# Another order and another cut of the sort in a graph-attention kernel: six groups, border steps moved, square roots issued earlier

## The chip, the cores and the metric

The kernel runs on one core of a Trainium2 chip. The metric is the device time of one execution in microseconds (us). The engines' names in the profile: PE is TensorE (PEld its weight loads), DVE is VectorE, ACT is ScalarE, POOL is GpSimd, SP is SyncE, which only issues DMAs here.

## What is computed

A graph with 6250 nodes of 96 values and 106,250 edges (both directions of 50,000, and a loop at each node), sorted by dst. For every edge the softmax-like weight of its four heads is computed and the weighted values are summed at the node `src`; then a layer norm.

```
q = (x[src] @ qW).reshape(e, 4, 24)
k = (x[dst] @ kW).reshape(e, 4, 24)
v = (x[dst] @ vW).reshape(e, 4, 24)
w = exp(clip(einsum('ehd,ehd->eh', q, k), -10, 10))
norms = segment_sum(w, src)[src]
res = segment_sum((w / (norms + 1e-8))[:, :, None] * v, src)
out = layernorm(x + (x + res))
```

## The kernel before

**Tiles.** Edges are wanted in order of src, cut into 49 blocks of 128 nodes. An edge tile is 128 edges of one block; `U` = 5 tiles make an iteration, and there are 176 iterations. In iteration m (function `tiles` of each engine, one after the other by hand) POOL has gathered the edges' k and v rows from the table `kv_table` in DRAM, one indirect DMA per tile (L475, five per iteration); PE turns a one-hot matrix (`ps_t`, L635), multiplies it with the block's q (`ps_q`, L609) and later the transposed one with the weighted values (`ps_r`, L623); DVE multiplies q by k (L1059), reduces (L1078), clips (L1086), weighs (L1068), builds the one-hot matrix (L1049) and adds to the block's sums (L1041); ACT takes the exponential (L720) and copies the one-hot matrices (L727, L733). The engines run one to two iterations apart. POOL may be ahead by `R` = 8 buffers and by `Y` = 6 results: before gather n it waits for `s_wv` at n - 7 and `s_res` at n - 5.

**The sort.** The gathers need the addresses `dst_s` of their edges, in the order of src. The 850 columns of 125 edges are sorted in groups of `GC` columns. Group g is sorted while the tile iterations of group g - 1 run. One group needs, in this order:
- ranking, mostly on DVE, in named pieces: `mark0` to `mark3` (49 comparisons, L800), `tally` (PE counts the marks, ACT copies), `pay` (L810 to L818), `pair0` to `pair2` (L824 to L830), `count` (waits for the tally's copies and for PE), `base`, `bounds`, `sel0` to `sel6` (L942, L946), `table`, `tree`, `own`, `choose` (choice matrices, L917 to L922);
- one sort unit per 10 columns: DVE makes three matrices (L982, L986, L988), ACT makes 10 rows of steps (L682, `TS[g]` + 1 wide), PE does 20 matmuls of that width (L595), one unit behind the other two;
- a border: ACT copies the two sums (L703, L704), DVE takes differences (L998), PE turns them (`turn`, L561, L564), ACT copies (L710), PE multiplies with the choice matrices (`pick`, L574 to L580), DVE makes the addresses (`pick`, L1008 to L1017) and tells POOL with `s_sorted`.

`plan()` writes one list, `PLAN`, and each engine follows it in its own program: an entry is an iteration (with sort units or without), or a piece, for which an engine does what it has under that name, or nothing. For group g >= 1 the list has some iterations with ranking pieces between them, then iterations with units in them, one iteration, `differ` (ACT's copies, DVE's differences), `turn`, one more iteration, `pick`. The last `pick` lies `LS[g-1]` iterations before the group's first tile. Group 0 is ranked and sorted before any tile iteration, while x is projected to q, k and v in seven pieces (`project`), with PE, ACT and the stores to `kv_table`.

With GC = 140, 110, 140, 190, 270 the step widths are 186, 205, 234, 283 and 361; groups begin at iterations 0, 17, 39, 66 and 103; ranking goes through 7, 9, 11 and 15 iterations and sorting through 7, 10, 14 and 20, with 11, 14, 19 and 27 units. From iteration 99 on there is tile work alone.

**The end.** When all is summed, POOL, DVE and ACT normalize: DVE computes the variances in four parts, ACT takes each root (L746), DVE the inverse (L1170), ACT writes output rows (L751).

## Time and profile before

| | us |
|---|---|
| median of 3 runs (lowest 1390.77, highest 1398.35) | 1392.9 |
| the profiled execution's own time | 1393.83 |
| its span, from the first to the last instruction | 1392.0 |
| busy: PE, DVE, POOL, ACT | 1074.6 (77%), 1012.9 (73%), 928.7 (67%), 690.1 (50%) |
| first and last gather (L475) issued | 97.6, 1350.0 |
| chain of work that ended last: DVE, POOL, ACT, issue, PE | 24%, 24%, 20%, 15%, 14% |

The chain is spread over four engines, so that it names no single limit. The rows further down show busy times stretch by stretch, and single instructions in order of time. A row of the table of stretches gives the stretch, its length, the busy time (and count) of PE, PEld, DVE, ACT and POOL, the granted share of TensorE's clock, the busy share of the DMA engines and GB/s. Its stretches are cut at the starts of the multiply L1059 of iterations 5, 12, 14, 23, 33, 35, 46, 60, 62, 77 and 97. A row of a timeline gives start, duration, engine, line, operation, out<-in, shapes, count, and in brackets the engine's idle time before it and what ended it. The span and the execution's own time differ by 1.8 us, which lie outside the instructions.

### The profile page before, as it was taken

What the parts mean: (1) busy time and instruction counts of PE and PEld (TensorE: products, weight loads), DVE (VectorE), ACT (ScalarE), POOL (GpSimd) and SP (SyncE); (2) the same over time, 40 slices, a digit from 0 to 9 for tenths busy, and PEclk for the clock granted to TensorE, in tenths of its full rate; (3) what the DMA queues carried; (4) which work ended last, traced back from release to release, by engine and by line L of the source; (5) the groups of instructions that cost most, each with busy time, mean ns of one, the idle gap of its engine ahead of it and who ended that gap; (6) DMA issues with size and microseconds to landing.
All of it is one profiled execution on the core that took longest, in us unless ns stands there. A gap on an engine that the chain in (4) does not pass through costs nothing.

```text
span 1392.0 us, 23222 instructions
## 1 busy us (share of the span) xinstructions
PE 1074.6 (77%) x6510; PEld 962.6 (69%) x6511; DVE 1012.9 (73%) x2885; ACT 690.1 (50%) x1464; POOL 928.7 (67%) x912
## 2 busy tenths in 40 slices
PE   7876777588777888876788988778888888888870
PEld 5755675577666778765677867677777777777760
DVE  7978887898699978588887777565555555555557
ACT  5842682269621699522289999232222222222224
POOL 1217775777677776567776657477777777777762
PEclk9985697669975689877579999885555555555555
DMA  5202222222222222222222212422222222222222
GB/s 157 80 12 78 69 69 59 74 69 68 64 65 68 67 68 65 55 61 77 69 67 57 63 53 66 117 78 79 77 79 79 77 78 79 77 78 79 79 66 69
DMA packets 68425, 100.58 MB, mean 72 GB/s; under 512 B 33528, under 2 KB 54005, under 8 KB 68335
## 3 DMA queue, kind: packets, MB, share of 16 engines
q0 software_dynamic: 42240, 86.56, 22.8%
q1 hardware_dynamic: 26094, 12.94, 3.4%
q8 instruction: 42, 0.69, 0.2%
q14 instruction: 49, 0.39, 0.1%
HBM read 92.23 MB, written 7.22 MB: 71 GB/s over the span
## 4 chain that ended last, share of the span: by engine, by line
DVE 24%; POOL 24%; ACT 20%; issue 15%; PE 14%; DVEq 2%; DMA 1%; SPq 0%; POOLq 0%; ACTq 0%
POOL kv L475 23%; ACT steps_m L682 14%; DVE acc L1041 4%; PE ps_r L623 3%; PE ps_q L609 3%; ACT oneh L733 3%; PE ps_a L595 2%; DVE place_m L942 2%; PE ps_b L595 2%; ACT onehT L727 2%; DVE place_m L946 2%; DVE prod L1059 2%; DVE steps_m L800 2%; DVEq L392 1%; DVE kb_m L933 1%
## 5 line engine op out<-in xcount | busy, mean ns | idle before, releaser
L475 POOL DMA_INDIRECT kv<-kv_table,dst_s x880 | 907.2, 1031 | 391.2 <-issue 353.7
L609 PE MATMUL ps_q<-qt,onehT 128*128 x1760 | 348.0, 369 | 101.6 <-ACT onehT L727 96.8
L609 PEld LDWEIGHTS ps_q<-qt,onehT 128*128 128x128 f32 x1760 | 318.9, 274 | 131.1 <-issue 129.0
L623 PE MATMUL ps_r<-wv,oneh 128*128 128x100 f32 x1752 | 353.1, 374 | 72.2 <-DVE wv L1068 71.2
L623 PEld LDWEIGHTS ps_r<-wv,oneh 128*128 128x128 f32 x1752 | 321.9, 278 | 92.4 <-DVE wv L1068 76.9
L682 ACT ACTIVATE steps_m<-iota_f,pos_t 125x361 f16<-125x361 f32 (+4 forms) x794 | 341.2, 523 | 15.9 <-PE ps_b L595 12.0
L1041 DVE TENSOR_TENSOR acc<-acc,ps_r 128x100 f32 x876 | 222.5, 254 | 69.4 <-issue 32.6
L595 PE MATMUL ps_a<-steps_m,place_m 125*128 125x361 f16 (+4 forms) x794 | 212.0, 302 | 60.4 <-ACT steps_m L682 57.9
L720 ACT ACTIVATE wv<-clipped 128x20 f32<-128x20 f32 x176 | 38.0, 216 | 426.3 <-DVE clipped L1086 421.2
L1059 DVE TENSOR_TENSOR prod<-ps_q,kv 128x480 f32<-128x480 f32 x176 | 115.1, 654 | 162.7 <-DMA kv<-kv_table,dst_s 159.3
L727 ACT ACTIVATE onehT<-ps_t 128x640 f32<-128x640 bf16 x176 | 123.2, 700 | 188.5 <-PE ps_t L635 183.3
L595 PE MATMUL ps_b<-steps_m,place_m 125*128 125x361 f16 (+4 forms) x794 | 211.2, 300 | 0.0
L595 PEld LDWEIGHTS ps_a<-steps_m,place_m 125*128 125x128 f16 x794 | 111.5, 140 | 77.0 <-issue 33.8
L733 ACT ACTIVATE oneh<-ohb 128x640 f32<-128x640 bf16 x176 | 161.9, 920 | 1.3 <-PE ps_r L623 1.3
L595 PEld LDWEIGHTS ps_b<-steps_m,place_m 125*128 125x128 f16 x794 | 112.3, 141 | 9.8
L1068 DVE TENSOR_TENSOR wv<-kv,wv 128x480 f32<-128x480 f32 x176 | 114.2, 649 | 5.9 <-ACT wv L720 3.5
L1078 DVE TENSOR_REDUCE score<-prod 128x20 f32<-128x480 f32 x176 | 113.6, 646 | 0.2
L635 PE MATMUL ps_t<-ident_bf,ohb 128*128 128x128 bf16 x880 | 109.6, 277 | 4.3 <-DVE ohb L1049 4.3
L982 DVE TENSOR_TENSOR place_m<-iota_s,pos_p 125x1280 f16<-125x1280 f16 x85 | 69.9, 823 | 50.3 <-PE ps_b L595 50.0
L635 PEld LDWEIGHTS ps_t<-ident_bf,ohb 128*128 128x128 bf16 x880 | 98.0, 144 | 6.9 <-DVE ohb L1049 5.3
L1049 DVE TENSOR_TENSOR ohb<-iota_t,loc_s 128x640 bf16<-128x640 bf16 x176 | 98.1, 557 | 0.0
L986 DVE TENSOR_TENSOR place_m<-place_m,pay_a 125x1280 f16<-125x1280 f16 x85 | 69.8, 821 | 1.9
(196 smaller groups left out, 645.3 us busy)
## 6 DMA issues: line engine op xcount, KB each, us to landing
kv<-kv_table,dst_s POOLq DMA_INDIRECT x880
kv_table<-kv SPq DMA_DIRECT2D x7, 672.0 KB, 3.7
acc<-in_x_dram SPq DMA_DIRECT2D x6, 336.0 KB, 5.5
steps_m<-in_x_dram SPq DMA_DIRECT2D x6, 336.0 KB, 5.4
out_dram<-kv SPq DMA_DIRECT2D x6, 336.0 KB
dst_i<-in_dst_dram SPq DMA_DIRECT2D x1, 415.0 KB
src_i<-in_src_dram SPq DMA_DIRECT2D x1, 346.7 KB
acc<-in_x_dram SPq DMA_DIRECT2D x1, 288.0 KB, 4.6
```

The costliest lines, as they stand in the source:

```text
L475: nc.gpsimd.indirect_dma_start(kv[:, nm, u, :], None, kv_dram, bass.IndirectOffsetOnAxis(ap=dst_s[:, n * U + u:n * U + u + 1], axis=0)).th ...
L595: mm = nc.tensor.matmul(ps[:, 0:w], lhs[:, vm, :, j], steps, start=first and j == 0, stop=last and j == SU - 1)
L609: last = nc.tensor.matmul(ps_q[nm % 2][:, u * D:(u + 1) * D], onehT[:, nm % 2, u * P:(u + 1) * P], qt[:, bass.ds(blks[u], 1), :].rearrange ...
L623: last = nc.tensor.matmul(to, oneh[:, nm % 2, u, :], wv[:, nm % 2, u, :], start=True, stop=True)
L635: last = nc.tensor.transpose(ps_t[nm % 2][:, u * P // 2:(u + 1) * P // 2].bitcast(bf16), ohb[:, nm % 4, :, u], ident_bf[:, :])
L682: last = nc.scalar.activation(theta[:, vm, j, 0:w], iota_f[0:EP, 0:w], ACT.Sign, scale=-1.0, bias=pos_t[:, bass.ds(v * SU + j, 1)])
L727: nc.scalar.activation(onehT[:, nm % 2, :], ps_t[nm % 2][:, 0:U * P // 2].bitcast(bf16), ACT.Copy).then_inc(s_oneT, 1)
L733: nc.scalar.activation(oneh[:, nm % 2, :, :], ohb[:, nm % 4, :, :].rearrange("p n u -> p u n"), ACT.Copy).then_inc(s_onf, 1)
L1041: nc.vector.tensor_tensor(at, at, from_ps, ALU.add).then_inc(s_acc, 1)
L1059: nc.vector.tensor_tensor(prod[:, nm % 2, :].rearrange("p (u d) -> p u d", u=U), ps_q[nm % 2][:, 0:U * D].rearrange("p (u d) -> p u d", u= ...
L1068: nc.vector.tensor_tensor(wv[:, nm % 2, :, 0:D].rearrange("p u (h d) -> p u h d", h=HEADS), kv[:, nm, :, D:2 * D].rearrange("p u (h d) -> ...
L1078: nc.vector.tensor_reduce(score[:, nm % 2, :], prod[:, nm % 2, :].rearrange("p (h d) -> p h d", d=DH), axis=AX.X, op=ALU.add).then_inc(s_s ...
```

## The change

`GC` becomes six groups, 140, 110, 130, 160, 160 and 150 columns, and `LS` gets a fifth entry. By the kernel's own formulas the step widths are then 186, 205, 225, 254, 254 and 244; groups begin at iterations 0, 17, 39, 64, 95 and 126 (176 in all, as before); ranking goes through 6, 8, 9, 12 and 12 iterations and sorting through 8, 11, 14, 17 and 17, with 11, 13, 16, 16 and 15 units. From iteration 122 on there is tile work alone. `NCH`, the number of chunks of 128 sort tiles, goes from 3 to 2, and `iota` from 385 to 257 columns.

At a border ACT's copies get a name of their own, `lower`, and stand ahead of the iteration's tile work; PE's `pick` is called `choice` and stands right behind the turn, ahead of the second iteration. DVE's parts stay where they are. `pay` is listed behind `pair2`. For group 0 `choose` stands behind all units instead of behind the first two, and the projections move: the first ahead of the tally, the second from behind `tally0` and `tally1` on. SP issues the larger part of the src load behind dst and x instead of ahead of them. At the end ACT takes the next part's root ahead of the last two output rows of a part.

```diff
--- before.py
+++ after.py
@@ -25,10 +25,10 @@
     SU = 10
     KD = 4
     L = 2
-    LS = (3, 4, 4, 4)
+    LS = (3, 4, 4, 4, 4)
     Y = 6
 
-    GC = [140, 110, 140, 190, 270]
+    GC = [140, 110, 130, 160, 160, 150]
     G = len(GC)
     assert sum(GC) == EC and all(c % SU == 0 for c in GC)
 
@@ -87,19 +87,17 @@
     def plan():
         def rank(g):
             return ([f"mark{i}" for i in range(4)] + [f"tally{r}" for r in range(len(ROUNDS[g]))]
-                    + ["pay", "pair0", "pair1", "pair2", "count", "base0", "base1", "bounds"]
+                    + ["pair0", "pair1", "pair2", "pay", "count", "base0", "base1", "bounds"]
                     + [f"sel{i}" for i in range(7)] + ["table", "tree", "own"])
 
-        project_after = {"mark3": ("lift",), f"tally{len(ROUNDS[0]) - 1}": (0,), "count": (1,), "base1": (2,),
+        project_after = {"mark3": ("lift", 0), f"tally{len(ROUNDS[0]) - 1}": (1,), "base1": (2,),
                          "table": (3, 4, 5, 6)}
         for name in rank(0):
             PLAN.append(("piece", name, 0))
             for i in project_after.get(name, ()):
                 PLAN.append(("piece", "lift", 0) if i == "lift" else ("piece", "project", i))
-        PLAN.append(("sort", 0, V0[0], V0[0] + 2))
-        PLAN.append(("piece", "choose", 0))
-        PLAN.append(("sort", 0, V0[0] + 2, V0[1]))
-        for name in ("differ", "turn", "pick"):
+        PLAN.append(("sort", 0, V0[0], V0[1]))
+        for name in ("choose", "lower", "differ", "turn", "choice", "pick"):
             PLAN.append(("piece", name, 0))
         m = -L
         for g in range(1, G):
@@ -108,7 +106,7 @@
             count = end - m - 2
             names = rank(g) + ["choose"]
             units = V0[g + 1] - V0[g] + 1
-            ranked = round(count * (12 * GC[g] + 1000) / (34 * GC[g] + 1000))
+            ranked = round(count * (105 * GC[g] + 12000) / (365 * GC[g] + 12000))
             at = shares(len(names), ranked)
             for k in range(ranked):
                 m = plan_iters(m, 1)
@@ -116,9 +114,10 @@
                     PLAN.append(("piece", name, g))
             at = shares(units, count - ranked)
             PLAN.append(("iters", m, g, [tuple(range(V0[g] + a, V0[g] + b)) for a, b in zip(at, at[1:])]))
+            PLAN.append(("piece", "lower", g))
             m = plan_iters(m + count - ranked, 1)
-            PLAN.append(("piece", "differ", g))
-            PLAN.append(("piece", "turn", g))
+            for name in ("differ", "turn", "choice"):
+                PLAN.append(("piece", name, g))
             m = plan_iters(m, 1)
             PLAN.append(("piece", "pick", g))
             assert m == end
@@ -409,13 +408,13 @@
             for i, w in enumerate((qW, kW, vW)):
                 sp.dma_start(w_all[:, i * D:(i + 1) * D], w).then_inc(s_w, 16)
             load_x(1, xc[:, 1], s_x[1])
-            sp.dma_start(src_i[:, GC[0]:EC], src_rows[:, GC[0]:EC]).then_inc(s_src[1], 16)
             sp.dma_start(dst_i[:, :], dst.rearrange("(p c) -> p c", c=EC)).then_inc(s_dst, 16)
 
             for i in (2, 3):
                 load_x(i, xc[:, i], s_x[i])
             sp.wait_ge(s_xpad, 1)
             sp.dma_start(xlast[0:LASTB, :], x[(NB - 1) * P:N, :]).then_inc(s_xl, 16)
+            sp.dma_start(src_i[:, GC[0]:EC], src_rows[:, GC[0]:EC]).then_inc(s_src[1], 16)
 
             kv_rows = kv_dram.rearrange("(i b p) d -> i p b d", p=P, b=PC)
             for i in range(NPC):
@@ -638,7 +637,7 @@
                 for sort in sorts:
                     unit(*sort)
 
-            follow(pe, tiles, unit, {"lift": transpose_x, "project": project, "count": count, "table": table, "turn": turn, "pick": pick,
+            follow(pe, tiles, unit, {"lift": transpose_x, "project": project, "count": count, "table": table, "turn": turn, "choice": pick,
                                      **{f"tally{r}": lambda g, r=r: tally(g, r) for r in range(max(len(r) for r in ROUNDS))}})
 
 
@@ -696,7 +695,7 @@
                                      (ps_a, ps_b)[r % 2][0:EP, 0:NB * (b - a)].rearrange("p (b k) -> p b k", b=NB),
                                      ACT.Copy).then_inc(s_tev, 1)
 
-            def differ(g):
+            def lower(g):
                 w = TS[g] + 1
                 act.wait_ge(s_bin, V0[g + 1])
                 wait(act, s_sorted, g)
@@ -737,16 +736,23 @@
                 for sort in sorts[1:]:
                     unit(*sort)
 
-            follow(act, tiles, unit, {"lift": copy_xt, "project": project, "differ": differ, "turn": turn,
+            follow(act, tiles, unit, {"lift": copy_xt, "project": project, "lower": lower, "turn": turn,
                                       **{f"tally{r}": lambda g, r=r: tally(g, r) for r in range(max(len(r) for r in ROUNDS))}})
 
             act.wait_ge(s_wv, NBT)
+            def root(j):
+
+                a, b = PARTS[j][0] * PC, PARTS[j][1] * PC
+                act.wait_ge(s_var, j + 1)
+                nc.scalar.activation(std[:, a:b], var[:, a:b], ACT.Sqrt).then_inc(s_std, 1)
+
+            root(0)
             for j, (a, b) in enumerate(PARTS):
-                act.wait_ge(s_var, j + 1)
-                nc.scalar.activation(std[:, a * PC:b * PC], var[:, a * PC:b * PC], ACT.Sqrt).then_inc(s_std, 1)
                 act.wait_ge(s_inv, j + 1)
                 for i in range(a, min(b, NPC - 1)):
                     for k in range(PC if i < NPC - 2 else HALF):
+                        if j + 1 < len(PARTS) and i == b - 1 and k == PC - 2:
+                            root(j + 1)
                         n = i * PC + k
                         last = nc.scalar.activation(yout[i][:, k, :], acc[:, n, 0:D], ACT.Identity,
                                                     scale=inv[:, n:n + 1], bias=shift[:, n:n + 1])
```

## Rows read from the trace of the kernel before

**Rows 1.** Table of stretches, cut at starts of L1059; columns as told above.
```profile
150.50:201.70 51.20, 39.64 (x348) 38.48 (x349) 46.73 (x105) 46.28 (x122) 41.14 (x34) 0.86 0.24 66
223.50:292.50 69.00, 45.99 (x255) 40.73 (x255) 62.83 (x226) 17.47 (x32) 53.21 (x52) 0.62 0.27 74
292.50:361.50 69.00, 56.67 (x502) 54.61 (x501) 62.92 (x143) 64.99 (x162) 55.10 (x46) 0.91 0.25 67
383.60:466.00 82.40, 60.68 (x305) 53.13 (x305) 75.11 (x248) 21.81 (x39) 63.92 (x58) 0.58 0.25 69
466.00:569.30 103.30, 88.76 (x688) 82.75 (x689) 87.09 (x199) 97.56 (x221) 74.00 (x66) 0.87 0.24 64
596.30:702.70 106.40, 74.64 (x414) 65.61 (x415) 94.67 (x280) 28.78 (x51) 79.37 (x78) 0.64 0.26 71
702.70:863.50 160.80, 140.10 (x996) 123.31 (x996) 124.79 (x282) 156.80 (x319) 105.68 (x97) 0.92 0.23 61
917.90:1340.00 422.10, 354.07 (x1681) 323.81 (x1682) 230.41 (x670) 116.90 (x203) 320.08 (x336) 0.52 0.28 78
```

**Rows 2.** Timeline of POOL: gathers 1, 86, 196 and 631 of 880.
```profile
97.62 1.22 POOL L475 DMA_INDIRECT kv<-kv_table,dst_s  x1 [45.03 <-issue]
...
223.65 0.94 POOL L475 DMA_INDIRECT kv<-kv_table,dst_s  x1 [8.11 <-DVE dst_s L1017]
...
383.74 0.95 POOL L475 DMA_INDIRECT kv<-kv_table,dst_s  x1 [5.83 <-DVE dst_s L1017]
...
1036.43 0.95 POOL L475 DMA_INDIRECT kv<-kv_table,dst_s  x1 [0.30 <-issue]
```

**Rows 3.** Timeline of the start, before the first tile iteration: DVE and PE.
```profile
14.59 0.23 DVE L810 TENSOR_SCALAR src_i<-src_i 125x140 int32<-125x140 int32 x1 [4.30 <-DMA dst_i<-in_dst_dram]
...
16.44 0.17 DVE L824 TENSOR_SCALAR rank_u<-bin_u 125x14 uint16<-125x14 uint16 x1
...
20.55 0.87 DVE L838 TENSOR_REDUCE cnt_f<-kst_m 125x49 f32<-125x686 f16 x1
...
21.70 0.20 PE L536 MATMUL ps_a<-cnt,tri_h 125*128 125x49 f16 x1 [1.73 <-DVE cnt L839]
...
51.09 1.58 DVE L917 TENSOR_SCALAR choice<-iota_f,where 128x138 f16<-128x138 f32 x1
...
90.63 0.35 DVE L998 TENSOR_TENSOR dif<-cum_a 128x185 f16<-128x185 f32 x1 [3.05 <-ACT cum_a L703]
```

**Rows 4.** Timeline of ACT in sort stretches: step rows and tile work.
```profile
348.06 7.71 ACT L682 ACTIVATE steps_m<-iota_f,pos_t 125x234 f16<-125x234 f32 x20
...
713.35 0.20 ACT L720 ACTIVATE wv<-clipped 128x20 f32<-128x20 f32 x1
...
714.88 4.96 ACT L682 ACTIVATE steps_m<-iota_f,pos_t 125x361 f16<-125x361 f32 x10
```

**Rows 5.** Timeline of DVE: an iteration with one sort unit.
```profile
749.13 0.65 DVE L1059 TENSOR_TENSOR prod<-ps_q,kv 128x480 f32<-128x480 f32 x1
...
750.77 0.26 DVE L1041 TENSOR_TENSOR acc<-acc,ps_r 128x100 f32 x1 [0.43 <-issue]
...
754.94 0.66 DVE L1059 TENSOR_TENSOR prod<-ps_q,kv 128x480 f32<-128x480 f32 x1
```

**Rows 6.** Timeline of the last border: PE and DVE.
```profile
868.35 0.34 PE L595 MATMUL ps_a<-steps_m,place_m 125*128 125x361 f16 x1 [2.03 <-ACT steps_m L682]
...
871.47 1.25 PE L609 MATMUL ps_q<-qt,onehT 128*128 x10
...
876.11 0.53 DVE L998 TENSOR_TENSOR dif<-cum_a 128x360 f16<-128x360 f32 x1 [7.81 <-ACT cum_a L703]
...
879.36 2.45 PE L609 MATMUL ps_q<-qt,onehT 128*128 x10
...
885.88 0.54 DVE L1008 CAST bits_b<-ps_b 128x365 int32<-128x365 f32 x1 [5.09 <-PE ps_b L577]
```

**Rows 7.** Timeline of the end: the last inverse on DVE.
```profile
1384.50 0.24 DVE L1170 RECIPROCAL inv<-std 128x14 f32<-128x14 f32 x1 [2.30 <-ACT std L746]
```

## Prediction

> **What bounds the kernel now.** The page shows no engine busy for more than 77% of the span, so the limit changes from stretch to stretch, and I read a table of stretches next [rows 1]. I cut it at the starts of the DVE multiply L1059, one per tile iteration. From 917.9 us on there is only tile work: 422.1 us for 336 gathers of L475, 1.256 us each, or 6.28 us per iteration of five, while DVE is busy 55% of it. GpSimd's issuing of gathers is the bound there. Before that the sort of the next group shares the engines. "Rank" stretches (223.5, 383.6, 596.3) are DVE's: it is busy 91, 91 and 89% of them. "Sort" stretches (150.5, 292.5, 466.0, 702.7) belong to DVE and ACT in the small groups (91% and 90%) and to ACT in the largest (98%), at 7.3, 6.9, 7.4 and 8.0 us per iteration (7, 10, 14, 20 iterations). Between them stand four borders of two iterations each: 21.8, 22.1, 27.0 and 26.6 us, from the gaps between those stretches, the last from 863.5 to 890.1.
>
> GpSimd's own rows [rows 2] say where it stands: it starts at 97.6, waits 8.11 us at the first border and 5.83 us at the second, and little else before 384 us. The gather with which iteration 126 begins starts at 1036.43. The change ends its last sort there, so I forecast that gather's start. Everything behind it, 50 iterations and the end, stays as it is.
>
> **The change part by part.** *Start.* Pair moves ahead of pay. Before, DVE waits 4.30 us for the dst load, then does pay, and pair from 16.44 to the count at 20.55 [rows 3]. Now pair's 4.1 us fill that wait, and dst lands earlier, as the second src load (346.7 KB) is issued behind it. The count could start 4.1 us earlier, but PE has the second projection queued ahead of it: seven copies at about 0.45 us and a transposed tile, after the tally's end at 15.8, put PE's count at about 19.5 instead of 21.70. Gain 2.2 us (bounds 0 and 4.1). The first projection goes ahead of the tally, into PE's idle time while DVE marks; it needs the second x tile and finishes at about the time at which the marks are done, cost 0 (up to 1). The choice matrices of group 0 (1.58 us the first, 2.2 in all, of a DVE that has no idle time there) move into the 3.05 us in which DVE waits before L998: gain 2.2. With the smaller iota and one chunk less, 0.3. Sum 4.7, so gathers start at 92.9.
>
> *Rank stretches.* Pure tile work without waiting for gathers takes 27.8 us for the 7 iterations between 890.1 and 917.9, where no sort runs and gathers lie ready, 4.0 each. Of 69.0 (9 iterations, 140 columns), 82.4 (11, 190) and 106.4 (15, 270) [rows 1] that leaves 33.0, 38.4 and 46.4 us of rank work, about 0.105 us per column. So 130 columns cost 31.9, 160 cost 35.2, 150 cost 34.1. With 6, 8, 9, 12 and 12 iterations: 48.5 (52.5 now, from 98, less one), 63.9, 71.2, 83.2, 82.1.
>
> *Sort stretches.* ACT needs 1.53 us for an iteration's tile work, and for ten step rows 4.9 us at 361 wide and 3.85 at 234 [rows 4]: 0.008 us per column. The new groups are 205, 225, 254, 254 and 244 wide: 3.6, 3.8, 4.0, 4.0, 3.9. DVE needs 5.4 for an iteration with one unit (749.13 to 754.94 less 0.43 idle [rows 5]) and 2.3 for each further one. Units and iterations are 11 in 8, 13 in 11, 16 in 14, 16 in 17, 15 in 17. The larger of the two engines is 50.1 (DVE), 65.9, 85.6, 90.2 (ACT), 87.2 (DVE). Today's stretches last 1.03 to 1.10 of their busier engine; with 1.06 (1.08 for the first) that is 54, 69.9, 90.7, 95.6, 92.4.
>
> *Borders.* Before, ACT copies the sums (L703) only after tile work that waits for PE, and DVE stands 7.81 us for it; then PE's tile work (2.45 us for L609 alone at 1.2 GHz, some 4.9 with the other two) lies between the turn and the pick, and DVE waits 5.09 us [rows 6]. After: copies straight after the last unit, pick straight after the turn. What waits behind them: behind ACT's copy, the exp and the copies of its tile iteration; behind PE's pick, which waits for ACT's turned copies about 1 us, its own tile work. Both are short of the waits that they remove. The second takes PE's 4.9 us out of the chain; by the first the copies could start when the last unit ends (871.47), about 4 us sooner, of which PE's tile work, until about 874.2, leaves 3 to the turn at 877.1. So I take 8 us less per border (bounds 3 and 12): 14, 14, 18, 18, 18. There is one border more.
>
> *Sum for the pipeline.* 92.9 and 0.4 to its first iteration, rank 348.9, sort 402.6, borders 82: iteration 122, where the last sort ends, at 927.
>
> *Sum for GpSimd.* Its own pace is the second limit. Free, five gathers take 6.26 us. In sort stretches a gather costs 1.21 and 1.20 us (41.14/34, 55.10/46) against 0.953 in the plain loop (320.08/336), 0.8 us per unit; in rank stretches the surplus is 3.6, 8.6 and 5.0 us. The Trainium skill ("GPSIMD Engine Reference", Key points) says that GpSimd shares its SBUF interfaces with VectorE and contends with DVE instructions that have two SBUF inputs; by this rule L1068 should lengthen gathers in the plain loop too, which the 0.953 does not show, so the rule bears out L986 and L988 alone. Group 1's 17 iterations took 117.9 us (97.6 to 215.5) and group 2's 22 took 154.3 (223.65 to 377.9); with one unit less, 153.5. For the 87 behind them: 545 free, 47 units at 0.8 are 38, three rank stretches at 5.7 are 17, and about 9 to 11 us in which it is too far ahead (it may lead by five iterations, and rank at 7.9 us per iteration fills that). From 92.9: 117.9, 153.5 and 610 give 975.
>
> The pipeline alone would be at iteration 122 at 927, 48 us before GpSimd is ready for 126: the sort no longer holds GpSimd, and GpSimd is late next. So the gather of iteration 126 starts at 975 instead of 1036.4, 61 us earlier. *End.* The square roots are issued two rows early: DVE's 2.30 us wait [rows 7] shrinks by two output rows of 0.37 us, and a little earlier by 0.3: 1 us. The profiled execution took 1393.8 us (span 1392.0), 0.9 above the median of the three runs. 1393.8 less 62 is 1332; I say 1331.
>
> **The rivals.** *One: the last sorts keep today's pace.* One unit per iteration may leave dependencies open that two hid. At 7.4 us for 48 iterations, 355 instead of 279, the pipeline is at 1003: 33 us gained, 1360 us. Today's 103.3 for 14 speaks for it, the 5.8 us iteration [rows 5] against. If also the borders don't shrink (40 us), it is at 1043 and nothing is gained: 1400. Borders alone not shrinking (967) would cost nothing against the forecast, as GpSimd is at 975.
>
> *Two, slower: PE falls to 1.2 GHz.* In the plain loop PE runs at a granted clock of 0.52 though it is busy 84%; in sort stretches 0.86 to 0.92 [rows 1]. The skill ("TensorE: Matmul & The Clock Gate", Part 1) says activity releases the throttle; how much, these rows leave open, and the thinner mix of the last groups lies between. At 1.2 GHz tile work takes 5.27 us of PE (354.07 over 67.2 iterations); a unit at 361 wide takes 3.1 (868.35 to 871.47 [rows 6]), so at 254 wide 2.2 at 2.4 GHz and 4.3 at 1.2. For the last three groups: 253 and 197, so 450 instead of 279, the pipeline at 1098, 62 us late: 1455. It beats the forecast's 975 once it adds 48 of its 171 us, about a quarter of the time at 1.2 GHz beyond the present share, and turns the sign at 109, two thirds.
>
> *Three: GpSimd is faster.* With no surplus from DVE in the last three groups (55 us) gathers would follow the pipeline: at the least 935 for iteration 126, about 1295. Half of that gives 1310.
>
> *Four: the sixth group's fixed work eats all.* Its rank and border cost 18.6+18 us besides columns; it is in the sum. Only if my 0.105 per column were wrong would it show, and the three stretches agree.
>
> **How the numbers follow.** Forecast 0.55 (1320 to 1345), rival one with short borders 0.17 (1345 to 1368), with long ones 0.06 (about 1400), rival two 0.06, between these and the forecast 0.04, rival three 0.12 (1295 to 1320). The range from 1311 to 1365 leaves out rival three's lower part and the two slow cases. About 0.5% is what a measurement of this kernel can tell from no change: faster 0.87, same 0.05, slower 0.08.
>
> **What would show it.** In the profile after: gathers from 93; gaps ahead of L475 on DVE's dst_s gone or below 3 us at the last three borders; DVE waiting for kv in L1059 within the last sort stretches; about 6.9 us per iteration there; ACT below 85% busy; borders of 14 to 18 us; the gather of iteration 126 near 975. Wrong if GpSimd still waits for dst_s at 900 us, or if the granted clock of the last sort stretches is near 0.5.

## The result, and the profile after

| | before | after |
|---|---|---|
| median of 4 runs, us | 1394.8 (1390.8 to 1398.4) | 1326.2 (1322.1 to 1329.7) |
| profiled execution: own time, span | 1393.8, 1392.0 | 1328.3, 1326.5 |
| first gather, gather of iteration 126 | 97.6, 1036.4 | 97.7, 971.5 |
| idle time of L475 / L474 put down to `dst_s` | 33.8 | none |

The ratio is 0.951, with a 95% interval of 0.947 to 0.955: 69 us less. Some lines have moved in the changed kernel: the gather is L474, the multiply L1065, ACT's step rows L681, PE's sort matmuls L594, the sums' copies L702 and L703, the differences L1004, the sort unit's matrices L988, L992 and L994.

The table of stretches of the changed kernel, cut at the starts of L1065 of iterations 4, 12; 14, 22, 33; 44, 58; 60, 72, 89; 103, 120; 122 and 175. The columns are those of [rows 1]: length, busy time (count) of PE, PEld, DVE, ACT, POOL, granted clock, share of the DMA engines, GB/s.

```profile
142.50:195.80 53.30, 44.04 (x390) 42.55 (x390) 49.53 (x114) 48.42 (x127) 42.63 (x36) 0.87 0.25 68
212.20:278.20 66.00, 42.55 (x243) 37.19 (x240) 59.18 (x215) 17.34 (x31) 50.55 (x51) 0.65 0.28 77
278.20:347.00 68.80, 60.35 (x505) 57.84 (x505) 63.74 (x151) 62.23 (x155) 52.63 (x46) 0.84 0.25 67
...
433.80:518.90 85.10, 75.05 (x640) 71.47 (x640) 79.87 (x190) 81.49 (x194) 67.41 (x59) 0.92 0.26 70
535.30:618.00 82.70, 58.01 (x348) 51.81 (x347) 75.10 (x255) 24.23 (x43) 64.42 (x61) 0.69 0.26 72
618.00:728.90 110.90, 91.57 (x743) 85.69 (x743) 90.08 (x220) 92.27 (x211) 87.13 (x79) 0.91 0.26 71
...
825.20:940.40 115.20, 92.00 (x723) 85.49 (x723) 88.49 (x216) 88.59 (x203) 90.22 (x83) 0.87 0.26 71
957.60:1289.60 332.00, 277.41 (x1319) 253.47 (x1319) 183.50 (x535) 91.04 (x158) 249.53 (x261) 0.52 0.28 78
```

"Rank" stretches (212.20, 535.30) are still DVE's, busy 90 and 91% of them. The early sort stretches (142.50, 278.20, 433.80) have DVE at 93, 93 and 94%: 6.7, 6.3 and 6.1 us per iteration. The last two (618.00, 825.20) are new: 6.5 and 6.8 us per iteration, with DVE at 81 and 77%, ACT at 83 and 77%, and GpSimd, whose issue gaps of 0.30 us per gather aren't counted, busy 1.10 and 1.09 us per gather. The plain loop behind 957.60 runs at 6.26 us per iteration, as before.

GpSimd's timeline, as in [rows 2]: the gathers with which iterations 0, 17 and 39 begin (17 and 39 are the first of a group), and that of iteration 126.

```profile
97.67 1.22 POOL L474 DMA_INDIRECT kv<-kv_table,dst_s  x1 [44.28 <-issue]
...
214.87 0.95 POOL L474 DMA_INDIRECT kv<-kv_table,dst_s  x1 [0.30 <-issue]
...
366.51 0.95 POOL L474 DMA_INDIRECT kv<-kv_table,dst_s  x1 [0.30 <-PE ps_r L622]
...
971.51 0.95 POOL L474 DMA_INDIRECT kv<-kv_table,dst_s  x1 [0.30 <-issue]
```

Before, the second and third of these had waited 8.11 and 5.83 us for `dst_s`; now each follows its predecessor at the issue gap.

The timeline of the start, as in [rows 3], here with PE's and ACT's rows that matter.

```profile
16.66 0.87 DVE L844 TENSOR_REDUCE cnt_f<-kst_m 125x49 f32<-125x686 f16 x1 [0.57 <-ACT kst_m L694]
...
20.19 0.19 PE L535 MATMUL ps_a<-cnt,tri_h 125*128 125x49 f16 x1
...
29.18 0.29 PE L543 MATMUL ps_a<-wafter,weigh_h 49*128 49x138 f16 x1 [4.58 <-DVE wafter L897]
...
47.73 0.41 ACT L668 ACTIVATE kv<-ps_r 128x288 f32<-128x288 f32 x1
...
53.87 0.55 DVE L984 TENSOR_TENSOR onehT<-oneh,pos_h 125x744 f16<-125x744 f16 x1 [3.94 <-PE ps_b L594]
...
91.35 0.36 DVE L1004 TENSOR_TENSOR dif<-cum_a 128x185 f16<-128x185 f32 x1 [2.08 <-ACT cum_a L702]
```

DVE counts at 16.66 instead of 20.55, and then the gain is used up: at 91.35 it takes the differences 0.7 us later than before, and the first gather starts at 97.67 as before. The section on the prediction says where it went.

ACT's step rows (as in [rows 4]), then DVE's multiply in iterations with one unit (as in [rows 5]): twice while gathers lie ready, twice later in the same stretch.

```profile
699.73 4.09 ACT L681 ACTIVATE steps_m<-iota_f,pos_t 125x254 f16<-125x254 f32 x10
...
645.01 0.65 DVE L1065 TENSOR_TENSOR prod<-ps_q,kv 128x480 f32<-128x480 f32 x1
...
650.51 0.66 DVE L1065 TENSOR_TENSOR prod<-ps_q,kv 128x480 f32<-128x480 f32 x1
...
701.13 0.66 DVE L1065 TENSOR_TENSOR prod<-ps_q,kv 128x480 f32<-128x480 f32 x1 [0.71 <-DMA kv<-kv_table,dst_s]
...
708.42 0.66 DVE L1065 TENSOR_TENSOR prod<-ps_q,kv 128x480 f32<-128x480 f32 x1 [1.61 <-DMA kv<-kv_table,dst_s]
```

Ten step rows of 254 columns cost 4.09 us (predicted 4.0). The iteration from 645.01 to 650.51 takes 5.50 us with no idle time of DVE; the one from 701.13 to 708.42 takes 7.29, and what DVE waits for at its end is the transfer of a gather: 1.61 us. In the last two sort stretches these waits sum to 16.2 and 21.8 us; in the first three there is none, and DVE's waits there, under 5 us in each, are mostly for PE.

The last border, as in [rows 6]: PE, ACT and DVE.

```profile
939.53 0.27 PE L594 MATMUL ps_b<-steps_m,place_m 125*128 125x244 f16 x1
...
939.84 0.37 ACT L702 ACTIVATE cum_a<-ps_a 128x244 f32<-128x244 f32 x1 [0.48 <-PE ps_b L594]
...
944.26 0.41 DVE L1004 TENSOR_TENSOR dif<-cum_a 128x243 f16<-128x243 f32 x1
...
947.56 0.60 PE L573 MATMUL ps_a<-choice,turned 128*128 128x250 f16 x2 [0.75 <-ACT turned L709]
...
949.07 2.44 PE L608 MATMUL ps_q<-qt,onehT 128*128 x10 [0.41 <-issue]
...
950.27 0.66 DVE L1065 TENSOR_TENSOR prod<-ps_q,kv 128x480 f32<-128x480 f32 x1 [5.28 <-issue]
```

ACT copies the sums 0.04 us after PE's last sort matmul has ended (939.80), DVE no longer stands before L1004 (7.81 us before), and the choice matmuls (L573) follow the turn with no tile work between, 0.75 us after it, when ACT's copy has ended. The wait has moved: the tile work of the second iteration now stands behind them, and DVE stands 5.28 us before L1065. The row names no releaser; L1065 starts once PE is at L608, the matmuls that make its q. The end, as in [rows 7]:

```profile
1318.77 0.24 DVE L1176 RECIPROCAL inv<-std 128x14 f32<-128x14 f32 x1 [1.53 <-ACT std L747]
```

### The profile page after: what moved, and what is told of

It is laid out like the page before. It is cut to its first block, busy times and chain, and to the rows that moved or that the text cites. A ratio compares the mean times of both kernels' runs of the same rounds, so it can differ in the third digit from the quotient of the medians.

```text
span 1326.5 us, 23177 instructions
## 1 busy us (share of the span) xinstructions
PE 1016.5 (77%) x6512; PEld 920.2 (69%) x6513; DVE 1027.9 (77%) x3029; ACT 662.4 (50%) x1469; POOL 935.0 (70%) x912
## 4 chain that ended last, share of the span: by engine, by line
POOL 29%; DVE 25%; issue 17%; ACT 12%; PE 12%; DVEq 3%; DMA 2%; POOLq 0%; SPq 0%; ACTq 0%
POOL kv L474 28%; ACT steps_m L681 8%; DVE acc L1047 4%; PE ps_r L622 3%; DVE prod L1065 2%; PE ps_q L608 2%; ACT oneh L732 2%; DVE steps_m L806 2%; DMA kv<-kv_table,dst_s 2%; DVE place_m L948 2%; DVEq L391 2%; DVE place_m L952 2%; PE ps_a L594 2%; PE ps_b L594 1%; ACT onehT L726 1%
## 5 line engine op out<-in xcount | busy, mean ns | idle before, releaser
L474 POOL DMA_INDIRECT kv<-kv_table,dst_s x880 | 913.5, 1038 | 319.4 <-issue 313.0
L622 PE MATMUL ps_r<-wv,oneh 128*128 128x100 f32 x1752 | 339.8, 363 | 101.0 <-DVE wv L1074 100.4
L608 PE MATMUL ps_q<-qt,onehT 128*128 x1760 | 332.5, 357 | 97.8 <-ACT onehT L726 90.8
L622 PEld LDWEIGHTS ps_r<-wv,oneh 128*128 128x128 f32 x1752 | 309.2, 269 | 122.1 <-DVE wv L1074 116.2
L608 PEld LDWEIGHTS ps_q<-qt,onehT 128*128 128x128 f32 x1760 | 303.5, 263 | 124.9 <-issue 124.5
L681 ACT ACTIVATE steps_m<-iota_f,pos_t 125x254 f16<-125x254 f32 (+4 forms) x794 | 311.2, 484 | 17.4 <-PE ps_b L594 10.6
L1065 DVE TENSOR_TENSOR prod<-ps_q,kv 128x480 f32<-128x480 f32 x176 | 115.3, 655 | 175.5 <-DMA kv<-kv_table,dst_s 164.7
L594 PE MATMUL ps_a<-steps_m,place_m 125*128 125x254 f16 (+4 forms) x794 | 185.2, 283 | 28.6 <-ACT steps_m L681 28.0
L594 PE MATMUL ps_b<-steps_m,place_m 125*128 125x254 f16 (+4 forms) x794 | 183.6, 280 | 0.0
L594 PEld LDWEIGHTS ps_a<-steps_m,place_m 125*128 125x128 f16 x794 | 112.3, 141 | 35.2 <-issue 16.0
L1074 DVE TENSOR_TENSOR wv<-kv,wv 128x480 f32<-128x480 f32 x176 | 114.3, 649 | 3.2 <-issue 2.2
L594 PEld LDWEIGHTS ps_b<-steps_m,place_m 125*128 125x128 f16 x794 | 112.8, 142 | 3.3
L1084 DVE TENSOR_REDUCE score<-prod 128x20 f32<-128x480 f32 x176 | 113.7, 646 | 0.2
L634 PEld LDWEIGHTS ps_t<-ident_bf,ohb 128*128 128x128 bf16 x880 | 92.4, 141 | 18.8 <-DVE ohb L1055 17.2
L1055 DVE TENSOR_TENSOR ohb<-iota_t,loc_s 128x640 bf16<-128x640 bf16 x176 | 98.8, 561 | 0.0
L988 DVE TENSOR_TENSOR place_m<-iota_s,pos_p 125x1280 f16<-125x1280 f16 x85 | 69.6, 819 | 8.7 <-PE ps_b L594 8.7
L992 DVE TENSOR_TENSOR place_m<-place_m,pay_a 125x1280 f16<-125x1280 f16 x85 | 69.7, 820 | 1.6
```

What stands on the lines that cost most here:

```text
L474: nc.gpsimd.indirect_dma_start(kv[:, nm, u, :], None, kv_dram, bass.IndirectOffsetOnAxis(ap=dst_s[:, n * U + u:n * U + u + 1], axis=0)).th ...
L594: mm = nc.tensor.matmul(ps[:, 0:w], lhs[:, vm, :, j], steps, start=first and j == 0, stop=last and j == SU - 1)
L608: last = nc.tensor.matmul(ps_q[nm % 2][:, u * D:(u + 1) * D], onehT[:, nm % 2, u * P:(u + 1) * P], qt[:, bass.ds(blks[u], 1), :].rearrange ...
L622: last = nc.tensor.matmul(to, oneh[:, nm % 2, u, :], wv[:, nm % 2, u, :], start=True, stop=True)
L634: last = nc.tensor.transpose(ps_t[nm % 2][:, u * P // 2:(u + 1) * P // 2].bitcast(bf16), ohb[:, nm % 4, :, u], ident_bf[:, :])
L681: last = nc.scalar.activation(theta[:, vm, j, 0:w], iota_f[0:EP, 0:w], ACT.Sign, scale=-1.0, bias=pos_t[:, bass.ds(v * SU + j, 1)])
```

## The experiments

All times in this section are medians; "before" and the ratios are those of runs on the same chip. Two parts of the change were first taken one by one.

**e1_groups_only**: the kernel before with the new cut alone.

```diff
--- before.py
+    LS = (3, 4, 4, 4, 4)
+    GC = [140, 110, 130, 160, 160, 150]
...
+            ranked = round(count * (105 * GC[g] + 12000) / (365 * GC[g] + 12000))
```

> The kernel before with the six groups and their share of ranking iterations alone; borders, start and end as before. If GpSimd sets the end (the forecast's theory), borders that are 8 us longer are hidden behind its gathers: the gather of iteration 126 at 971 to 985, time 1326 to 1340 us. If the five borders stand in the sum, it is 40 us later: about 1366. If the groups alone bring nothing: 1393.

1338.5 us (1335.0 to 1341.1) against 1395.6, ratio 0.959 (0.957 to 0.962). The gather of iteration 126 there:

```profile
979.80 0.94 POOL L475 DMA_INDIRECT kv<-kv_table,dst_s  x1 [0.30 <-issue]
```

Its borders are long, 20.1, 22.5, 23.6, 16.8 and 18.5 us (changed kernel: 16.4, 15.5, 16.4, 13.2, 17.2), and iteration 122 starts at 968.3 instead of 957.6. Yet GpSimd is at iteration 126 at 979.8, 8.3 us later than in the changed kernel, and 2.8 of these it has from its start at 100.5. So 57 of the 69 us come from the cut; how the other 12 divide among borders, end and the scatter of single executions wasn't tried. That the borders can be 23 us longer in sum for 5.5 us of GpSimd's time says that GpSimd, and not the chain of the sort, is the limit there.

**e2_order_only**: the changed kernel with the old five groups.

```diff
--- after.py
+    LS = (3, 4, 4, 4)
+    GC = [140, 110, 140, 190, 270]
...
+            ranked = round(count * (12 * GC[g] + 1000) / (34 * GC[g] + 1000))
```

> The changed kernel with the five old groups; new order at borders, start and end. The old last group keeps ACT and DVE in front of GpSimd, so here shorter borders should show in full: four times 8 us, the gather of iteration 103 at about 860 instead of 890.6, time about 1362 us (1355 to 1370). If the order is worth nothing of its own: 1390 to 1394.

1367.3 us (1364.2 to 1368.6), ratio 0.980 (0.979 to 0.982). The gather with which the last group begins, iteration 103, started at 890.6 before:

```profile
861.42 0.94 POOL L474 DMA_INDIRECT kv<-kv_table,dst_s  x1 [3.17 <-DVE dst_s L1023]
```

Four borders of 15.3, 15.7, 19.8 and 19.6 us, where 21.8, 22.1, 27.0 and 26.6 stood: 6.4 to 7.2 us each, and GpSimd still waits for `dst_s` there. With long groups the borders are on the path, and the shorter ones are worth 28 us; with short groups they are mostly behind GpSimd. The two parts, 57 and 28, therefore give 69 together, not 85.

**The lost gain of the start.** The rows above suggest two steps: PE stands 4.58 us before L543, for DVE, and projections 3 to 6 stand behind it (as they did before), so that their last copy ends at 48.1 instead of 47.1; the first sort units of ACT and PE stand behind these, and DVE stands 3.94 us before its third unit. In the kernel before, this same wait had been filled with the choice matrices, whose first L917 took 1.58 us.

The traces also show why these four projections end later although PE begins them 1.1 us earlier (29.48, before 30.59). Before, PE had projections in hand up to L544 and never stood still there; now it has run out of them. Stretches of the kernel before and of the changed kernel, columns as in the table of stretches:

```profile
30.50:34.90 4.40, 4.40 (x29) 3.58 (x26) 4.23 (x6) 3.58 (x9) 0.75 (x1) 1.00 0.63 195
...
29.30:33.87 4.57, 4.57 (x19) 3.65 (x18) 4.37 (x7) 1.90 (x4) 0.00 (x0) 0.50 0.00 0
```

Behind its wait of 4.58 us PE runs at a granted clock of 0.50, its lower level of 1.2 GHz, for 4.6 us, in which it does 19 matmuls instead of 29; then the clock is 1.00 again. The four projections take 18.2 us instead of 16.1. In e3, with one projection moved into the gap, the clock stays at 1.00 from 24 to 42 us. Two runs on the two steps.

**e4_choose_back**: `choose` of group 0 again behind two units.

```diff
--- after.py
-        PLAN.append(("sort", 0, V0[0], V0[1]))
-        for name in ("choose", "lower", "differ", "turn", "choice", "pick"):
+        PLAN.append(("sort", 0, V0[0], V0[0] + 2))
+        PLAN.append(("piece", "choose", 0))
+        PLAN.append(("sort", 0, V0[0] + 2, V0[1]))
+        for name in ("lower", "differ", "turn", "choice", "pick"):
```

> The changed kernel with group 0's choice matrices back behind the first two units. Theory: they fall into DVE's 3.94 us wait before unit 2, so the first gather starts at 97.0 to 98.0 and the time stays (within 1 us). If moving them was worth its 2.2 us: first gather at 99.9, time 2.2 us longer.

1326.1 us (1325.1 to 1328.7), ratio 0.951 (0.949 to 0.953), first gather at 97.6. The move of the choice matrices is worth nothing. POOL and DVE in its timeline:

```profile
49.07 4.19 POOL L464 MEMSET acc<- 128x4900 f32 x1
49.72 3.62 DVE L925 TENSOR_SCALAR choice<-iota_f,where 128x138 f16<-128x138 f32 x1
```

The first choice matrix takes 3.62 us here and 0.29 in the changed kernel. It ends at 53.34, 0.08 us after GpSimd's clearing of `acc`; even so long, it fits into the wait of 3.94 us.

**e3_projections**: one projection more ahead of the wait.

```diff
--- after.py
-        project_after = {... "base1": (2,),
-                         "table": (3, 4, 5, 6)}
+        project_after = {... "base1": (2, 3),
+                         "table": (4, 5, 6)}
```

> The changed kernel with the projection of piece 3 moved from behind the table to behind base1. Theory: the start's 4.7 us were lost because the copies of the last projections on ACT end at 48.0 and unit 0 waits for them (DVE waits 3.94 us before unit 2). With piece 3 in the gap where PE waits 4.6 us for the bounds, the copies end near 44, the first gather starts at 94 instead of 97.7, and the time is 3 to 4 us shorter, about 1322.5. If DVE alone bounds the start: no change.

1328.8 us (1326.7 to 1331.4), ratio 0.953 (0.951 to 0.954), first gather at 98.7: not a microsecond gained. ACT's last copy ends at 42.25, even earlier than the 44 expected, but then (timelines of ACT, POOL and DVE):

```profile
41.84 0.41 ACT L668 ACTIVATE kv<-ps_r 128x288 f32<-128x288 f32 x1
...
42.31 0.75 POOL L457 COPY qt<-kv 128x672 f32<-128x672 f32 x1 [2.45 <-ACT kv L668]
43.00 4.18 POOL L462 MEMSET acc<- 128x4900 f32 x1
...
42.48 4.79 DVE L966 TENSOR_SCALAR src_i<-tmp_i 125x140 int32<-125x140 int32 x1
```

L966, 140 numbers per partition, takes 0.23 us in the changed kernel, with no POOL instruction beside it; here it starts beside a copy of POOL's and ends at 47.27, within 0.1 us of the end of the clearing of `acc` that follows that copy (43.00 and 4.18). The clearing comes as soon as the projections are done, and so, the earlier they are done, the worse a place it falls on. The theory "DVE is held by the clearing" was put to a run of its own, further down (e11).

**e5_three_gathers**: from iteration 8 on only three of the five gathers of an iteration are issued, so two fifths of the rows of k and v are stale ones; all other work stays.

```diff
--- after.py
-                    for u in range(U):
+                    for u in range(U if n < R else 3):
...
-                        dve.wait_ge(s_kv[nm], (n - nm) * (16 * U // R) + 16 * U)
+                        dve.wait_ge(s_kv[nm], (n - nm) * (16 * 3 // R) + 16 * U)
```

> The changed kernel with three gathers instead of five per iteration from iteration 8 on, so that two tiles of each iteration use old rows; all other work stands. It takes GpSimd off the path and shows the other engines' own time. Forecast's sum for them: iteration 122 at 931 us (927 and the 4 that the start did not gain), against 957.6 in the changed kernel; sort stretches of the last three groups at 6.5, 5.6 and 5.4 us per iteration; the plain loop at 4.0, so the end near 1195. If the other engines set the pace of the sort stretches themselves, those stay at 7.0 to 7.2 us per iteration and iteration 122 at about 957.

1262.7 us is a single execution. It ran on another chip (below), on which iteration 4 starts 28.5 us later (171.0), so I read differences within it: from iteration 4 to 122 it takes 759.3 us, the changed kernel 815.2. Its last two sort stretches, to be set against 618.00 and 825.20 above:

```profile
645.40:736.90 91.50, 84.95 (x719) 79.58 (x719) 89.28 (x220) 87.92 (x208) 52.31 (x49) 0.94 0.21 55
828.00:918.30 90.30, 81.93 (x702) 76.21 (x701) 87.25 (x216) 83.53 (x200) 54.98 (x49) 0.95 0.21 56
```

5.38 and 5.31 us per iteration instead of 6.5 and 6.8, with DVE at 98 and 97%. That is what the sort itself asks for when GpSimd is out of the way; in the changed kernel the rest is waiting for gathers. Between iterations 4 and 122 the forecast's chain alone takes 785 us (927 less 141.8, the sum of 92.9, 0.4 and 48.5), 26 more than here: 12.8 of them lie in the sort stretches (402.6 forecast, 389.8 measured) and 12.7 in the borders (82, 69.3); the rank stretches agree (300.4, 300.1).

**e6_two_inputs, e7_one_input, and again as e9_two_inputs_again, e10_one_input_again, with e8_after_again**, the changed kernel itself, as their base. If GpSimd sets the pace, DVE may have 50 us more to do for nothing, unless its work lengthens the gathers. One added instruction per sort unit of groups 1 to 5, with two SBUF inputs or with one:

```diff
--- after.py (e6, e9: behind L988)
+                if g:
+                    link(nc.vector.tensor_tensor(spare[:, :, :], iota_s[0:EP, :, :], spread(pay_a), ALU.mult))
--- after.py (e7, e10: behind L988)
+                if g:
+                    link(nc.vector.tensor_reduce(spare_f[:, :], iota_t[0:EP, :, :].rearrange("p n u -> p (n u)"),
+                                                 axis=AX.X, op=ALU.add))
```

> The changed kernel with one more DVE instruction per sort unit of groups 1 to 5, of the form of L992 (two SBUF inputs, 16 bits, 1280 elements), written to a spare tile; the result is not used. 71 units. If GpSimd sets the pace and these instructions lengthen gathers by 0.4 us per unit each: 20 to 30 us longer, the mean gather of the sort stretches from 1.10 to 1.14 us up by about 0.06. If DVE sets the pace: 0.8 us per unit, 57 us longer.

> As the kernel with one more two-input instruction, but with a reduce of 640 elements over a constant tile, one SBUF input, about 0.7 us. If GpSimd sets the pace and only two-input instructions of 16 bits lengthen gathers: 0 to 6 us longer. If DVE sets the pace: 0.7 us per unit, 50 us longer. If any DVE work beside a gather lengthens it: as with two inputs.

1521.6 and 1533.8 us, ratios 0.949 (0.947 to 0.952) and 0.957 (0.954 to 0.960). The chip was another one, on which the kernel before takes 1603.5 us. POOL's timeline of e6 in the plain loop shows what is different there:

```profile
1206.48 1.19 POOL L476 DMA_INDIRECT kv<-kv_table,dst_s  x1 [2.83 <-issue]
```

Most gathers follow at 1.25 us, but in the plain loop 22 of 233 come 2.2 to 3.1 us after their predecessor's end, 2.65 on average, instead of 0.30. The changed kernel itself wasn't run there, and the order of the two is the opposite of what either theory expects: inconclusive. So both were run again, with the base beside them, on a chip where the kernel before takes 1395.6 us.

> The changed kernel itself, unaltered, as the base for the two runs with an added DVE instruction. On a chip like the first: 1326 (1322 to 1331), ratio to before 0.951. On a chip where the kernel before takes about 1600 us, both theories expect a larger time of the changed kernel too, since its plain loop is gathers alone.

> Adds to each of the 71 sort units of groups 1 to 5 one DVE instruction of the form of L992 (two SBUF inputs, 1280 fp16 elements, 0.82 us) whose result nobody uses. DVE's work grows by 58 us, all of it before iteration 122. Theory (GpSimd's pace is the bound there, and a gather issued beside such an instruction is about 0.5 us longer): most of the 58 us lies in DVE's own slack, but some 60 more gathers are longer: 20 to 30 us more than the unaltered changed kernel of this call. Rival (DVE and ACT set the pace of the sort stretches): 50 to 60 us more.

> The same places as the run before it, but the added DVE instruction has one SBUF input (a reduce of 640 elements, about 0.7 us) and a single result per partition. DVE's work grows by 50 us. Theory: 0 to 8 us more than the unaltered changed kernel of this call, as gathers aren't longer beside it. Rival (DVE sets the pace): 45 to 55 us more.

| | us | ratio (interval) | to e8 |
|---|---|---|---|
| e8_after_again | 1328.6 (1324.1 to 1331.2) | 0.951 (0.948 to 0.953) | |
| e9_two_inputs_again | 1350.2 (1349.3 to 1351.4) | 0.967 (0.965 to 0.970) | +21.6 |
| e10_one_input_again | 1332.3 (1326.1 to 1334.8) | 0.953 (0.950 to 0.956) | +3.6 |

The groups of the gather, from the first to that of iteration 126 (count, busy us, mean ns), of e8, e9 and e10, and below them the stretch from iteration 103 to 120 of e8 and e10:

```profile
L474 POOL DMA_INDIRECT kv<-kv_table,dst_s x630 | 681.9, 1082 | 236.1 <-issue 229.3 <-DVE wv L1074 4.3 <-PE ps_r L622 2.4
...
L476 POOL DMA_INDIRECT kv<-kv_table,dst_s x631 | 703.7, 1115 | 236.5 <-issue 225.5 <-PE ps_r L624 5.8 <-DVE wv L1078 5.2
...
L476 POOL DMA_INDIRECT kv<-kv_table,dst_s x631 | 679.6, 1077 | 241.7 <-issue 235.0 <-PE ps_r L624 3.4 <-DVE wv L1079 3.0
...
825.60:943.10 117.50, 91.78 (x721) 85.05 (x721) 88.90 (x217) 88.11 (x201) 92.21 (x84) 0.89 0.27 71
...
834.70:945.40 110.70, 90.98 (x714) 85.11 (x715) 100.12 (x231) 87.64 (x201) 85.71 (x83) 0.86 0.28 74
```

The added instructions are equally long in sum: 57.9 us (71 of 815 ns) in e9, 57.5 (71 of 809 ns) in e10. In e10 DVE is busy 11 us more in the last stretch (100.12 to 88.90), which itself is no longer for it (110.70, e8 117.50). In the first three sort stretches DVE did set the pace: they take 59.1, 74.3 and 92.1 us instead of e8's 53.8, 67.4 and 85.4, and iteration 60 starts 9.3 us later (543.9, 534.6). By iteration 120 that is 2.4 us (945.4, 943.1): it was given back, since GpSimd had been the later one. Of the 58 us added 3.6 show, less than single executions differ. In e9 the gathers take some 21 us more (703.7, with one gather more in the window, against 681.9), and the kernel 21.6: GpSimd's time and the kernel's agree within a microsecond. Of the gathers between 200 and 960 us that start while e9's added instruction runs (48), every one is long, 1.51 us on average; of those that start beside e10's (21), none is, 0.95.

**e11_late_clear**: e3, and GpSimd clears `acc` when DVE has written the positions.

```diff
--- e3_projections.py
             pool.wait_ge(s_prj, NB)
+            pool.wait_ge(s_pos, 1)
             nc.gpsimd.memset(acc[:, :, :], 0.0).then_inc(s_acc0, 1)
```

> The run with projections 2 and 3 behind base1, and GpSimd clears acc (L462) only when DVE has written the positions of group 0 (s_pos). Theory (the DVE instruction L966 of the earlier run was held 4.8 us by the clearing of acc beside it): L966 takes 0.23 us again, the clearing falls beside the units' tensor_tensor instructions without lengthening them, the first gather starts at 94 instead of 97.7 and 98.7, and the time is 3 to 4 us below the unaltered changed kernel of this call, 1322.5 on a chip like the first. Rival (what held L966 was something else, such as ACT's copies or a transfer): L966 is still held, and the first gather starts at 98 or later.

1323.8 us (1320.6 to 1326.6), ratio 0.948 (0.946 to 0.951). Timelines of DVE and POOL:

```profile
43.45 0.67 DVE L967 TENSOR_SCALAR src_i<-tmp_i 125x140 int32<-125x140 int32 x1
...
45.68 0.82 DVE L989 TENSOR_TENSOR place_m<-iota_s,pos_p 125x1280 f16<-125x1280 f16 x1
...
43.28 0.75 POOL L457 COPY qt<-kv 128x672 f32<-128x672 f32 x1 [2.45 <-ACT kv L669]
45.31 4.19 POOL L463 MEMSET acc<- 128x4900 f32 x1 [1.28 <-DVE pos_t L972]
96.05 1.23 POOL L475 DMA_INDIRECT kv<-kv_table,dst_s  x1 [46.55 <-issue]
```

The instruction that took 4.79 us (now L967) takes 0.67, beside a copy of POOL's, and ends 0.09 us after it; the clearing falls beside the units' L985 and L989, which take their usual 0.55 and 0.82 us (45.22 to 45.77 the first L985). The first gather starts at 96.05, where e8, same chip, has 99.85 and e3 98.70. I had expected 94; DVE's table (L905, 41.38) was 1.0 us later than in e3, as starts differ by 1.5 us and more from one execution to the next (the count of L844 lies at 16.66 in the changed kernel, at 18.15 in e8, the same code). 3.8 us of start, and 4.9 us of time against e8: that is about what was expected, and the lowest median of all versions that do the whole work. But against the changed kernel's first median (1326.2) it is 2.4 us, and the intervals of the two ratios (0.946 to 0.951, 0.948 to 0.953) overlap. That DVE is held by the clearing is shown by the rows; that this version is faster by 0.3% is likely, not shown.

## Why the prediction was right, and where it was not

*What bounds it: right.* GpSimd took over as the limit. The forecast put the gather of iteration 126 at 975; it started at 971.5. The time follows, 1331 to 1326.2 (the profiled execution: 1332 to 1328.3).

*Start: wrong, the whole gain of 4.7 us.* The step that failed is "The choice matrices ... of a DVE that has no idle time there" together with the 2.2 us from pair ahead of pay. Of the latter 1.5 were there at PE's count (20.19, forecast 19.5, before 21.70). That DVE was never idle before 53 us was only true because those choice matrices filled the time in which ACT and PE were still projecting, and their 1.58 us was no cost of their own either: L917 takes 0.28 to 0.29 us where no clearing runs beside it. The start hangs on a second chain, projections, ACT's copies, first units, which I costed at nothing. It ended 1 us later than before: projections moved ahead left PE idle for 4.58 us before L543, and behind that it ran 4.6 us at a granted clock of 0.50. Both gains ended in DVE's wait of 3.94 us. e4 shows the second term at 0. e11 shows that the start can give 2 to 4 us, once that chain and the clearing of `acc` are out of the way. How much of the start the lower clock alone costs wasn't tried by itself.

*Rank stretches: right.* Behind the first (48.5 forecast; 44.4 measured, from 98.1 to iteration 4: the iteration taken off was worth 8 us, not 4), 63.9, 71.2, 83.2 and 82.1 were forecast, 66.0, 71.3, 82.7 and 83.1 measured. 0.105 us per column holds.

*Sort stretches.* 54, 69.9 and 85.6 to 90.7 for the first three, measured 53.4, 68.8 and 85.1: the busier engine's sum without the 6% on top would have been enough for the third. The last two, 95.6 and 92.4, measured 110.9 and 115.2. That isn't the sort: e5 has 91.4 and 90.3 there. They are stretched by GpSimd, as the forecast's own 6.9 us per iteration says. "Iteration 122 at 927" was the time of a chain alone, never to be seen in the kernel, where 957.6 stands, and by e5 it was 26 us too long. GpSimd being the later one, this error didn't reach the time.

*Borders: right in size, less in worth.* 16.4, 15.5, 16.4, 13.2 and 17.2 for 14, 14, 18, 18, 18. e2 shows 6.4 to 7.2 us for each where I took 8. The price that I gave for the tile work behind the pick was also paid: DVE's 5.28 us before L1065.

*GpSimd's pace: right, a little high.* Groups 1 and 2 took 117.2 and 151.6 us (forecast 117.9, 153.5), the 87 iterations behind them 605.0 (forecast 610). Table of stretches for POOL alone, of the changed kernel, cut at the gathers that begin iterations 39, 64, 95 and 126 (length, busy (count), clock, DMA, GB/s):

```profile
366.50:543.90 177.40, 134.13 (x126) 0.80 0.26 71
543.90:760.90 217.00, 169.78 (x155) 0.79 0.26 72
760.90:971.50 210.60, 163.38 (x155) 0.75 0.32 85
```

Against 0.95 us per gather these have 54 us too much in sum; 55 was forecast (38 for units and 17 for ranking). The term that was mis-sized is the time in which GpSimd is too far ahead: 9 to 11 us. Beyond the usual 0.30 us between two gathers it stands still for 5.2 us in all, ahead of four gathers between 398 and 432 us, and in e8 and e4 nowhere behind iteration 39. So the two errors, 4.8 us of start too early and 7.6 us of GpSimd too slow, partly cancel: part of the closeness of 975 to 971.5 is luck.

*End.* From the gather of iteration 126 to the end of the span it takes 355.0 us instead of 355.6: 0.6, forecast 1; the wait before the last inverse is 1.53 us instead of 2.30.

*The rivals.* One, today's 7.4 us per iteration in the last sorts: the stretches took 6.5 and 6.8, and 5.3 to 5.4 in e5. Two, PE at 1.2 GHz: the granted clock is 0.91 and 0.87 in these stretches. Three, GpSimd without its surplus: it has all of it. Four, the fixed work of the sixth group: it is there, rank stretches of 82.7 and 83.1 us, and GpSimd covers it.

*The surplus of the gathers: the size right, one reading wrong.* The Trainium skill ("SBUF — State Buffer", section "Who interferes with whom") says that a tensor_tensor with both inputs in SBUF contends with GpSimd's reads and a tensor_reduce on trn2 never does. e9 and e10 agree (1.51 and 0.95 us per gather beside them). The prediction read the plain loop's 0.953 us per gather as a sign that the fp32 L1068 doesn't lengthen them, so that the rule holds for the 16-bit L986 and L988 alone. The traces don't bear that out. In the plain loop before, 66 gathers start beside L1068, but with at most 0.24 us of it left; the longest takes 1.06 us. Between 200 and 960 us of the changed kernel 64 start beside L1074 (the same multiply), and all 8 that take more than 1.15 us start with 0.36 to 0.52 us of it left. What counts is the rest of the instruction when the gather starts, not its type: the last section has the rows.

## What to carry over

When the sum of a chain and the pace of a producer are both worked out, forecast the later of the two at the point where they meet, and look for the next microseconds in the one that wins: here 58 us of work added to DVE cost next to nothing (e10), but not as long instructions with two SBUF inputs (e9). An engine that is never idle may only be covering a wait for another chain; ask of every "no idle time" what ran beside it. Work moved ahead on an engine can leave a hole where it stood, and PE paid for that hole twice, with its length and with the lower clock behind it. And a long clearing on GpSimd, though nobody waits for it, has to be placed where no one-input DVE instruction meets it.

## What the runs showed of the hardware

*A gather that starts beside a DVE tensor_tensor with both inputs in SBUF is held until that instruction ends, whatever its type.* Timelines of POOL and DVE in the changed kernel:

```profile
643.56 1.44 POOL L474 DMA_INDIRECT kv<-kv_table,dst_s  x1 [0.30 <-issue]
...
643.37 0.82 DVE L992 TENSOR_TENSOR place_m<-place_m,pay_a 125x1280 f16<-125x1280 f16 x1
...
527.94 0.65 DVE L1074 TENSOR_TENSOR wv<-kv,wv 128x480 f32<-128x480 f32 x1
528.12 1.29 POOL L474 DMA_INDIRECT kv<-kv_table,dst_s  x1 [0.31 <-issue]
```

Alone a gather takes 0.95 us. These two end at 645.00 and 529.41, 0.81 and 0.82 us after the end of L992 (fp16) and of L1074 (fp32). Between 200 and 960 us 176 gathers start more than 0.03 us after the start of such an instruction (L992, L994, L988, L952, L1055, L1074 and others, of fp16, bf16, uint16 and fp32) with more than 0.13 us of it left, and 173 of them end 0.80 to 0.84 us after its end. Of the 31 that start within the first 0.03 us, 29 take their usual 0.95. Beside DVE's multiply with q in PSUM (L1065) 44 of 47, and beside the reduce L1084 all 37, take less than 1.15 us. L992 and L994 lengthen gathers most (59 of 59, 1.50 us on average) because they are the longest, 0.82 us. From iteration 64 to 126 the gathers take 38.7 us more than 0.95 each (22.6 and 16.1 us for 31 iterations each); 33.3 of these fall on gathers held so, 17.7 on L992 and L994. That is 0.7 and 0.5 us per iteration, nearly the whole difference between 6.26 and GpSimd's 7.0 and 6.8 there.

*A DVE tensor_scalar is held by GpSimd's memset*: 4.79 us instead of 0.23 in e3, 3.62 instead of 0.29 in e4, and L917 in the kernel before, 1.58 us instead of 0.28, until the clearing that began at 48.39 ends (52.58). tensor_tensor instructions beside the same clearing keep their length (e11). The Trainium skill (the same section) says that tensor_scalar can enter a mode in which it and GpSimd exclude each other for a whole instruction, and tensor_tensor cannot; the trace agrees with both.

*PE's granted clock fell to 0.50 behind a wait of 4.58 us* in the changed kernel's start and came back to 1.00 after 4.6 us; in the plain loop it is 0.52 with PE busy 84%.

*Chips can differ by 15% on this kernel.* The kernel before took 1395.6 us on two chips and 1603.5 on a third. In e6 and e7, traced on that third chip, most gathers take the same 0.95 us, but nearly every tenth of the plain loop (22 of 233, 23 of 240) comes 2.2 to 3.1 us after the one before it, where 0.30 is usual. What makes it wait wasn't tried.
